# Self attention's projections in 16-bit float pairs, with scales found during cross attention, and the last FFN statistics ahead of the last products

## The reference, cut to what matters

```python
x = x + xattn(_layernorm(x), ctx, mask, rms_scale, q_w, kv_w, out_w)  # 4 heads of 128; keys and values from ctx (1601 rows)
x = x + attn(_layernorm(x), WQ, WK, WV, WO)                           # 16 heads of 32, causal, 64 rows
x = x + ffn(_layernorm(x), W_fc, ln_w, ln_b, W_proj)                  # ternary weights, GELU, layer norm over 2048
```

```python
def heads(W): return (x @ W).reshape(B, S, 16, 32).transpose(0, 2, 1, 3)
Q, K, V = heads(WQ), heads(WK), heads(WV)
score = einsum('bhqd,bhkd->bhqk', Q, K) / sqrt(32) + causal_mask
out = einsum('bhqk,bhkd->bhqd', softmax(score), V)
return out.reshape(B, S, E) @ WO
```

## Time and profile before

| | us |
|---|---|
| median of 3 runs | 1065.26 |
| the profiled execution, time | 1066.37 |
| the profiled execution, span of its trace | 1064.4 |
| PE busy / PEld busy | 930.7 / 700.7 |
| DVE busy / ACT busy / POOL busy | 668.4 / 505.0 / 375.6 |

### The profile page before, as it was taken

How to read it: one execution, slowest core, us unless ns; L and a number is a source line. 1 busy time by engine, 2 the same in 40 slices (tenths; PEclk the granted TensorE clock), 3 DMA queues, 4 the chain that set the end, 5 groups by cost and what they waited for, 6 DMA issues and landing times. The chain is left out here.

```text
span 1064.4 us, 22549 instructions
## 1 busy us (share of the span) xinstructions
PE 930.7 (87%) x7307; PEld 700.7 (66%) x7307; DVE 668.4 (63%) x1334; ACT 505.0 (47%) x1059; POOL 375.6 (35%) x506
## 2 busy tenths in 40 slices
PE   3798879898888888878979999999889999999996
PEld 2787667686676776657968887888765444444443
DVE  5577756766766777676366566766656538475543
ACT  4565445654455554544333333433446455555542
POOL 3354444444444444440022111211103325444434
PEclk9899989999999999988989999999989999999998
DMA  6621223211222322331355543444422102012011
GB/s 178 184 76 56 80 88 86 87 54 57 76 86 73 97 74 76 115 115 41 90 160 140 149 126 108 127 124 108 118 60 76 55 1 88 32 40 70 21 60 43
DMA packets 100318, 93.02 MB, mean 87 GB/s; under 512 B 45424, under 2 KB 61904, under 8 KB 100176
## 3 DMA queue, kind: packets, MB, share of 16 engines
q1 hardware_dynamic: 99376, 90.96, 29.2%
q10 hardware_dynamic: 672, 0.26, 0.1%
q0 software_dynamic: 128, 0.03, 0.0%
HBM read 74.37 MB, written 12.66 MB: 82 GB/s over the span
## 5 line engine op out<-in xcount | busy, mean ns | idle before, releaser
L255 PE MATMUL bank<-f,f 128*128 128x256 f32 (+4 forms) x5032 | 637.8, 300 | 68.8 <-issue 26.0
L255 PEld LDWEIGHTS bank<-f,f 128*128 128x128 f32 (+3 forms) x5032 | 460.9, 160 | 196.5 <-issue 80.8
L244 DVE TENSOR_TENSOR f<-bank,f 128x512 fp32r<-128x512 f32 x211 | 140.5, 683 | 47.7 <-ACT f L241 45.8
L241 ACT ACTIVATE f<-bank 128x512 fp32r<-128x512 f32 x211 | 121.1, 591 | 88.8 <-PE bank L230 83.6
L230 PE MATMUL bank<-f,f 128*128 128x128 f32 x896 | 132.5, 279 | 33.7 <-DVE f L244 13.0
L230 PEld LDWEIGHTS bank<-f,f 128*128 128x128 f32 x896 | 102.9, 143 | 56.1 <-issue 31.3
L1248 PE MATMUL bank<-f,f 128*128 128x512 f16 x512 | 123.1, 384 | 0.0
L1221 POOL TENSOR_TENSOR f<-f,f 128x512 f32<-128x512 f32 x59 | 75.1, 1273 | 132.9 <-ACT f L1216 132.9
L1226 DVE SCALAR_TENSOR_TENSOR f<-bank,f,f 128x512 f16<-128x512 f32 x64 | 48.0, 750 | 92.0 <-ACT f L1208 75.8
L463 POOL TENSOR_TENSOR f<-f,f 128x512 f32<-128x512 f32 x32 | 42.0, 1311 | 160.9 <-ACTq L75 138.9
L954 POOL TENSOR_TENSOR f<-f,f 128x512 f32<-128x512 f32 x32 | 33.4, 1043 | 177.4 <-DVE f L951 177.4
(11 more groups left out here) (138 smaller groups left out, 995.6 us busy)
## 6 DMA issues: line engine op xcount, KB each, us to landing
f<-in_ctx_dram SPq DMA_DIRECT2D x71, 256.0 KB, 2.8
f<-x_scratch SPq DMA_DIRECT2D x64, 256.0 KB, 3.8
x_scratch<-f SPq DMA_DIRECT2D x32, 256.0 KB, 2.0
f<-in_L_ffn_W_fc_dram SPq DMA_DIRECT2D x32, 256.0 KB, 2.9
f<-in_L_ffn_W_proj_dram SPq DMA_DIRECT2D x32, 256.0 KB, 3.4
f<-in_x_dram SPq DMA_DIRECT2D x31, 256.0 KB, 2.9
f<-in_ktab_dram SPq DMA_DIRECT2D x71, 64.0 KB, 2.0
f<-f SPq DMA_DIRECT2D x64, 64.0 KB, 2.4
```

What stands on the lines that cost most here:

```text
L241: return maybe("act", lambda e: e.activation(hi, src, ACT.Copy), sem(name + "_hi"), waits, when)
L244: return maybe("dve", lambda e: e.tensor_tensor(lo, src, hi.bitcast(F32), ALU.subtract), sem(name + "_lo"), waits, when)
L255: f = lambda e, i=i, a=a, b=b: e.matmul(dst, a, b, start=(first and i == 0), stop=(last and i == n - 1), skip_group_check=check)
```

## The change

Self attention's four weights, its turned x tiles (`XT`) and its attention output (`ET2`) become pairs of `float16`. A weight is first divided by its largest magnitude `m`, so that its low part stays in range: `hi = f16(w/m)`, `lo = w/m - hi`. Q and K are multiplied by `m` when they are copied from PSUM (`scale=wis` on an instruction that is there already); V stays scaled, and WO's product is multiplied by `m_V * m_O` in `store`, which adds the residual.

To find `m` each weight is loaded once more during cross attention, at slots 24, 38, 52 and 66, into `wo_t`. Four VectorE reductions in the slots s+4 to s+7 give the largest magnitude of each partition; it is written to DRAM (s+9), read back to all partitions (s+11), and reduced again and inverted (s+13). The split of a weight takes `scale=` on ScalarE, and on VectorE a scalar_tensor_tensor in place of a tensor_tensor; `store` takes a scalar_tensor_tensor too. The places in SBUF are laid out anew. The numbers of matmuls and their columns stay as they are.

At the end of the FFN the last group's statistics come before all products of the last two steps, the sums of squares first, and these products are then made row tile by row tile.

```diff
     for i in range(3):
-        Wh[i], Wl[i] = early(4, D, dt=F32R), early(4, D, dt=F32R)
-    XT = [early(2, 4, 256, dt=F32R), early(2, 4, 256, dt=F32R)]
+        early.at = CONST + (24576, 32768, 57344)[i]
+        Wh[i], Wl[i] = early(4, D, dt=F16), early(4, D, dt=F16)
+    XT = [early(2, 4, 256, dt=F16), early(2, 4, 256, dt=F16)]
-    Wh[3], Wl[3] = outs(4, D, dt=F32R), outs(4, D, dt=F32R)
+    Wh[3], Wl[3] = outs(4, D, dt=F16), outs(4, D, dt=F16)
-    ET2 = [late(4, 128, dt=F32R), late(4, 128, dt=F32R)]
+    ET2 = [late(4, 128, dt=F16), late(4, 128, dt=F16)]
...
+    def s2_wfetch(i):
+        w = (WK, WQ, WV, WO)[i]
+        tok["ws", i] = dma(wo_t[:, :, :], w.rearrange("(c p) n -> p c n", p=128), "s_wst",
+                           [*(tok["wm", i - 1] if i else ()), *tw1["o"]])
+    def s2_wmax(i, c):
+        t = op("dve", lambda e: e.tensor_reduce(wmc[:, c:c + 1], wo_t[:, c, :], AX.X, ALU.max, apply_absolute_value=True),
+               sem("s_wm"), [tok["ws", i]])
+        if c == 3:
+            t = op("dve", lambda e: e.tensor_reduce(wmx[:, i:i + 1], wmc[:, :], AX.X, ALU.max), sem("s_wm"), [t])
+            tok["wm", i] = [t]
+    def s2_wout(i):
+        tok["wo", i] = dma(wmaxd[i:i + 1, :].rearrange("a (p n) -> (a p) n", n=1), wmx[:, i:i + 1], "s_wmo", tok["wm", i])
+    def s2_wback(i):
+        tok["wb2", i] = dma(back[:, i, :], wmaxd[i:i + 1, :].to_broadcast([128, 128]), "s_wmb", [tok["wo", i], tok["tq"]])
+    def s2_wscale(i):
+        D_ = lambda f, w: op("dve", f, sem("s_wm"), w)
+        t = D_(lambda e: e.tensor_reduce(wis[:, i:i + 1], back[:, i, :], AX.X, ALU.max), [tok["wb2", i]])
+        t = D_(lambda e: e.tensor_scalar(wis[:, i:i + 1], wis[:, i:i + 1], 1.0e-30, None, ALU.max), [t])
+        t = D_(lambda e: e.reciprocal(wsc[:, i:i + 1], wis[:, i:i + 1]), [t])
...
     def s2_wsplit(i, after, c):
-        tW[i] = split("s_W2", raw_w(i)[:, c, :], Wh[i][:, c, :], Wl[i][:, c, :],
-                      [tok["w", i], *after()], [tok["w", i]])
+        th = op("act", lambda e: e.activation(hi, src, ACT.Copy, scale=wsc[:, i:i + 1]), sem("s_W2_hi"),
+                [tok["w", i], tok["wsc", i], *after()])
+        tl = op("dve", lambda e: e.scalar_tensor_tensor(lo, src, wsc[:, i:i + 1], hi, ALU.mult, ALU.subtract),
+                sem("s_W2_lo"), [th, tok["w", i], tok["wsc", i]])
+    def halves(name, src, hi, lo, w_hi, w_lo=()):
+        th = op("act", lambda e: e.activation(hi, src, ACT.Copy), sem(name + "_hi"), w_hi)
+        return th, op("dve", lambda e: e.tensor_tensor(lo, src, hi, ALU.subtract), sem(name + "_lo"), [th, *w_lo])
...
-        to = op("dve", lambda e: e.tensor_tensor(xo[:, u, :], bank[k][:, :], xr[:, u, :], ALU.add),
+        to = op("dve", lambda e: e.scalar_tensor_tensor(xo[:, u, :], bank[k][:, :], wsc[:, 4:5], xr[:, u, :],
+                                                        ALU.mult, ALU.add),
...
-        tok["qk", u] = [op("act", lambda e: e.activation(o, bank[k][:, 0:256], ACT.Copy), sem("a_QK"),
+        tok["qk", u] = [op("act", lambda e: e.activation(o, bank[k][:, 0:256], ACT.Copy, scale=wis[:, w:w + 1]), sem("a_QK"),
...
+    for i in range(4):
+        s = 24 + 14 * i
+        at(s, 9, lambda i=i: s2_wfetch(i))
+        for c in range(4):
+            at(s + 4 + c, 2.95, lambda i=i, c=c: s2_wmax(i, c))
+        at(s + 9, 9, lambda i=i: s2_wout(i))
+        at(s + 11, 9, lambda i=i: s2_wback(i))
+        at(s + 13, 2.95, lambda i=i: s2_wscale(i))
...
     def s3_plast():
-        for t in (2, 3):
-            s3_p(last - 1, [t])
         for t in range(4):
-            s3_p(last, [t])
+            for q in (last - 1, last):
+                s3_p(q, [t])
...
-        w = [*tok["acc", g], *tok["acc2", g], *gfree[k], t_on]
-        for t in range(4):
-            for z in range(2):
+        w = {1: [*tok["acc2", g], *gfree[k], t_on], 0: tok["acc", g]}
+        for z in (1, 0):
+            for t in range(4):
...
-    at(H0 + last + 2, 2.1, lambda: s3_p(last - 1, [0, 1]))
```

More of the change, by code:

```diff
@@ L166, in few @@
 def few(nc, handle, bank, base, x1d, x2d, x, ctxd, mask, rms, qw, kvw, ow, WQ, WK, WV, WO, Wfc, lnw, lnb,
-        Wproj, cosk, sink, cosq, sinq, identd, causald, out, picked, kmask, ktab, plan, nb=B):
+        Wproj, cosk, sink, cosq, sinq, identd, causald, out, picked, kmask, ktab, plan, wmaxd, nb=B):
     ni = nb // 2
@@ L754, in few @@
     for i in range(3):
-        Wh[i], Wl[i] = early(4, D, dt=F32R), early(4, D, dt=F32R)
-    XT = [early(2, 4, 256, dt=F32R), early(2, 4, 256, dt=F32R)]
+        early.at = CONST + (24576, 32768, 57344)[i]
+        Wh[i], Wl[i] = early(4, D, dt=F16), early(4, D, dt=F16)
+    early.at = CONST + 73728
+    XT = [early(2, 4, 256, dt=F16), early(2, 4, 256, dt=F16)]
+    early.at = CONST + 90112
     xa, xn = early(2, D), early(2, D)
-    Wh[3], Wl[3] = outs(4, D, dt=F32R), outs(4, D, dt=F32R)
+    Wh[3], Wl[3] = outs(4, D, dt=F16), outs(4, D, dt=F16)
     WO_raw = outs(4, D)
@@ L777, in few @@
     mrow, mdiag, isc, sc, lsc = const(2), const(2), const(2), const(2), const(2, 16)
+    wmc, wmx, wis, wsc = const(4), const(4), const(4), const(5)
+    back = Region(CONST + EARLY + 72704, CONST + EARLY + 74752)(4, 128)
     tok, tW = {}, {}
@@ new lines, in s2_wout @@
+    def s2_wout(i):
[7 more added lines that the diff above has]
+        t = D_(lambda e: e.reciprocal(wsc[:, i:i + 1], wis[:, i:i + 1]), [t])
+        if i == 3:
+            t = D_(lambda e: e.tensor_tensor(wsc[:, 4:5], wis[:, 2:3], wis[:, 3:4], ALU.mult), [t])
+        tok["wsc", i] = t
@@ L872, in ln_T @@
         tok["xnT", i] = [tt]
-        tok["XT", i] = split("n_XT", dst, dsth, dstl, [tt, *free])
+        tok["XT", i] = halves("n_XT", dst, dsth, dstl, [tt, *free])
         give(k, tok["XT", i])
@@ L878, in store @@
         u, j = i % 2, i % ni
-        to = op("dve", lambda e: e.tensor_tensor(xo[:, u, :], bank[k][:, :], xr[:, u, :], ALU.add),
-                sem("n_xo"), [tk, tok["xr", i], *tok["late"], *d2("ost", i - 2)])
+        to = op("dve", lambda e: e.scalar_tensor_tensor(xo[:, u, :], bank[k][:, :], wsc[:, 4:5], xr[:, u, :],
+                                                        ALU.mult, ALU.add),
+                sem("n_xo"), [tk, tok["xr", i], tok["wsc", 3], *tok["late"], *d2("ost", i - 2)])
         tok["out", i] = [to]
@@ L901, in s2_qk @@
         o = (QT, KT)[which][:, u % 2, c, :]
-        tok["qk", u] = [op("act", lambda e: e.activation(o, bank[k][:, 0:256], ACT.Copy), sem("a_QK"),
-                           [tk, *tW[w], *tok["early"], *d2("sc", 2 * u - 3)])]
+        tok["qk", u] = [op("act", lambda e: e.activation(o, bank[k][:, 0:256], ACT.Copy, scale=wis[:, w:w + 1]), sem("a_QK"),
+                           [tk, tok["wsc", w], *tW[w], *tok["early"], *d2("sc", 2 * u - 3)])]
         give(k, tok["qk", u])
@@ L1002, in s2_ET @@
         tok["enT", i] = [tt]
-        tok["ET", i] = split("a_ET", dst, ET2[0][:, :, :], ET2[1][:, :, :], [tt, *tok["late"], *d2("o2", i - 1)])
+        tok["ET", i] = halves("a_ET", dst, ET2[0][:, :, :], ET2[1][:, :, :], [tt, *tok["late"], *d2("o2", i - 1)])
         give(k, tok["ET", i])
@@ L1281, in s3_stat @@
                         bank[k][:, z * 4 + t:z * 4 + t + 1], a, ones[:, 0:1], start=n == 0, stop=n == m,
-                        skip_group_check=True), sem("f_p") if t == 3 and z and n == len(parts) - 1 else None,
-                        w if t + z == 0 else ())
+                        skip_group_check=True), sem("f_p") if t == 3 and not z else None,
+                        w[z] if t + n == 0 else ())
         tok["stat", g] = [tk]
@@ L2452, in program @@
         places = nc.dram_tensor("tile_rows", (B, FT), I32, kind="Internal").ap()
+        wmaxd = nc.dram_tensor("weight_max", (4, 128), F32, kind="Internal").ap()
         handles = []
@@ L2476, in program @@
                identd, causald, out)
-        short, prep, steps, ahead, begun = few(nc, semaphores(8), bank, base, x1d, x2d, *ins, picked, kmask, ktab, plan)
+        short, prep, steps, ahead, begun = few(nc, semaphores(8), bank, base, x1d, x2d, *ins, picked, kmask, ktab, plan,
+                                               wmaxd)
         long = every(nc, semaphores(0, begun), bank, base, x1d, x2d, *ins)
```

3 lines of the change are left out of this document (added).

## The result

The changed kernel takes 1072.91 us (median of 4 runs, 1071.1 to 1073.77); the kernel before, on the same chip, 1064.98 (4 runs, 1063.77 to 1065.47). The ratio is 1.0074, 95% interval 1.0056 to 1.0091: slower by 0.7%, where 1055.4 us, 0.9% faster, was forecast. The profiled execution took 1072.21 us with a span of 1070.1.

A forecast was written before the change was run, and what follows sets the result against it. TensorE, the busiest engine in every stretch, was taken as the bound, by its own pace in self attention's steady part. Profiled 1066.4 - 12.2 + 3 - 0.7 = 1056.5 us, median 1.1 lower: 1055.4 us, range 1050 to 1062.5.

The forecast's parts named there:

- What self attention's matmuls save: Self attention: float16 starts 0.108 and 0.216 us apart; 8.4 us (bounds 0 and 8.4) with 256 columns, 6.9 with 512.
- the 15.3 us: Self attention: TensorE time saved by float16 matmuls with 256 and 512 columns together, bounds 6.9 and 15.3.
- the 1067.6: Time by the skill's pace formula, self attention already at its floor and nothing gained; under a rival with chance 0.10.
- How much arrives: Self attention: half of the ramp's saving, nine tenths of the steady part's 12.3 us, less 0.4 at half clock: 12.2 us.
- the ramp: Start of self attention, 484 to 556 us: half of 3.0 us saved counts, 1.5 us, since other engines' chains hold TensorE.
- ScalarE's `scale=`: Scaling put on existing ScalarE instructions in self attention: adds no instruction, so no cost was counted.
- the lower bound: Self attention's least arriving gain, with 512 columns alone and the same shares: 5 us.
- What the search costs: Cross attention: 14.2 us of added VectorE work, mostly hidden, costs 3 us (bounds 0 and 14.2); transfers cost 0.
- The trip through DRAM: Cross attention: write, landing and read back hidden, 3.2 us for the read against 7 us of lead; cost 0.
- rival (c): Cross attention: late SP transfers make the inversion hold VectorE four times; at 4 us each, 1071 us; chance 0.06.
- Rival (b): Cross attention: VectorE's new work lands on TensorE's path nearly in full, 12 us of 14.2, giving 1064.4; chance 0.08.
- The end: End of the FFN: statistics start about 0.7 us sooner, gaining 0.7 us (bounds 0 and 0.75).

The follow-up runs named there:

- e2: The kernel before plus the search alone, its result unused, with float32r pairs and the old end: 1077.02 us, ratio 1.0110.
- e6: The kernel before with only the new order of its end: 1064.69 us beside 1064.62, ratio 0.9997.
- e1: The changed kernel without the search (no second load, reductions or trip through DRAM), scales set by constants: 1057.05 us, 0.9919 of the kernel before.
- e4: The changed kernel with second load and reductions but no write, read back or inversion, scales constant: 1060.09 us, 0.9948 of the kernel before.
- e5: The changed kernel with second load and trip through DRAM but no reductions, writing a constant 0.25: 1062.75 us, 0.9967 of the kernel before.
- e7: The changed kernel with only the inversion moved, from s+13 to s+19: 1063.84 us, 0.9972 [0.9956, 0.9987] of the kernel before.
- e0: The changed kernel itself, unaltered, timed again in another comparison: 1067.28 us, 1.0019 of the kernel before.
- e9: The changed kernel with the read back moved to s+22 and the inversion to s+32: 1062.77 us, 0.9967 of the kernel before.
- e16: The changed kernel without the search, scales constant, run again in a later comparison: 1058.13 us, 0.9932 of the kernel before.
- e15: The changed kernel without the search, scales constant, and with the old end: 1057.03 us, 0.992 of the kernel before.
- e3: The changed kernel with the read back moved to s+14 and the inversion to s+19: 1063.44 us, 0.9979 of the kernel before.
- e11: e4 plus the four writes of 128 x 4 bytes to DRAM, nothing read back: 1060.67 us, 0.9962 of the kernel before.
- e10: The changed kernel without the trip, maximum over partitions by TensorE transpose and matmul in slot 84: 1066.83 us, 1.0015 of the kernel before.

## Why the prediction was wrong, step by step

**What self attention's matmuls save: right.** 0.109 and 0.216 us against 0.108 and 0.216. The choice between the bounds 0 and 8.4 us for 256 columns was right, and with it the 15.3 us. The formula of the Trainium skill ("TensorE: Matmul & The Clock Gate", Back-to-back issue gap), which is given there for isolated matmuls, 109 and 216 ns, agrees with these rows for `float16`; for `float32r` it did not. The time lies nearer to the 1067.6 by it than to my forecast, but by luck: the paces did fall as forecast, and what took the gain away is the search.

**How much arrives: the share was too high, and the half clock takes part of it.** 12.2 us were forecast and 0.7 for the end; 8.9 arrived from slot 127 to the end in the profiled execution, and that holds the new end. Behind slot 127 the kernel before has 43.3 us at half clock and the changed one 48.1, so up to 2.4 of the 4.0 missing us are clock. It isn't chance alone: every one of the fifteen traces with `float16` pairs has a half-clock stretch of 3.4 us some 26 to 28 us behind slot 127 (after: from 517.1), and none of the three with `float32r` (before, `e2`, `e6`) has one there. What stands ahead of it is a wait for the high half of a weight, 2.1 us in the fifteen and 1.7 in the three.

The kernels with fixed scales give 0.9919 and 0.9932 in all, 7.2 to 8.6 us. I had written that a wait behind a transpose "moves with TensorE" and doesn't eat what was saved. The waits in the twelve tiles grew from 15.1 to 19.9 us instead. My reading is that such a wait is a chain of fixed length through ScalarE and VectorE, partly covered by TensorE's products that stand between transposes and use: the products got shorter, the chain didn't (the two halves of such a split take 0.59 and 0.68 us on ScalarE and VectorE before and after). Only 1.4 of the 4.8 us stand in rows that name a split, though; for the 2.3 in the row "issue" the cause isn't shown. The share was 6.6 of 11.5, not nine tenths.

In the ramp, from slot 127 to the scores of the second tile, I counted 1.5 us and nothing arrived (86.5 us before, 87.0 after), with 19.7 us at half clock before and 24.1 after: the difference, 2.2 us when halved, is more than what was forecast there.

ScalarE's `scale=` was priced at nothing because it "adds no instruction"; it does make the instructions longer. The copies of Q and K, before and after:

```profile
L902 ACT ACTIVATE f<-bank 128x256 f32<-128x256 f32 x64 | 24.3, 380 | 81.9 <-PE bank L255 81.3
```

```profile
L945 ACT ACTIVATE f<-bank,f 128x256 f32<-128x256 f32 x64 | 30.0, 469 | 75.8 <-PE bank L255 75.8
```

That is 0.09 us for each of 64, and as much for each high half of a weight (0.62 to 0.71 us); the low half takes 0.83 us on VectorE instead of 0.69, where 0.06 more was forecast. What of it reaches TensorE isn't shown.

One sum of this step is wrong, without consequence: the lower bound, 512 columns alone with these shares, is 0.4 + 5.4 - 0.4 = 5.5 us and not 5.

**What the search costs: the step that failed.** It was priced at 3 us: 16 reductions and four inversions at 0.15 us each, the transfers at nothing. Measured, the search costs 10.7 us alone (`e2`), and the changed kernel's ratios, 1.0019 and 1.0074, stand 0.0100 and 0.0155 above `e1`'s 0.9919: 10.7 to 16.5 us. Three terms stand in its place.
- The reductions: 10.9 us of VectorE as forecast, and `e4` less `e1` is 0.0029, 3 us (`e4`'s waits: +3.6). Forecast were 2.4 us (16 x 0.15), so this term was about right.
- The trip through DRAM, its transfers taken as hidden and priced at nothing: +4.6 us of TensorE's waits (`e5`). I had written "cost 0, and if that cover is gone, VectorE stands and waits, with all behind it". The cover was gone. I counted one landing, the read's 3.2 us, against 7 us of lead; the write lands 8.2 us (median) after its issue and the read 4.1 after its own, and SP waits in between. At the worst place the read back went out at 314.50 and VectorE stood waiting for it from 318.73 - 2.50 = 316.23: 1.7 us of lead, not 7. Moving the inversion alone by six slots (`e7`) took 3 to 4 us of waits away and brought the ratio from 1.0019 to 0.9967. This is rival (c)'s mechanism, with a smaller size at VectorE (4.8 us in all) than its price of 4 us for each of four.
- The half clock, not forecast in cross attention at all: up to 4.6 us between the two profiled executions (half of 23.7 - 14.4). The worst stall, 4.06 us with 6.8 us at half clock, goes with a late landing of the write (9.5 us); where it landed after 7.4 the wait was 1.62 us and the clock stayed full (`e0`).

Rival (b)'s 12 us came out as a total, but not by its mechanism: the reductions cost a quarter of it.

**The end: right in the trace, nothing in the time.** The statistics moved by 0.73 us and the end of the span by 0.6; neither pair of kernels shows it in the time, where less than 0.2% can't be told apart.

**What stays open.** `e9` has no wait of VectorE for the read back and still stands 0.0031, 3 us, above `e4`, with +1.7 us of TensorE's waits; write and read alone cost no more than the intervals allow. Whether the remainder is the sum of small terms or the half clock's placement wasn't settled. The second load was never run alone. Nor was it settled why the changed kernel differs by half a per cent between two comparisons, beyond the landing and the half clock named above.

The best version is the one with fixed scales (`e1`, `e16`, with the old end `e15`): 0.992 to 0.993 of the kernel before. It gives up that the scale follows the weights. Of those that find the magnitudes themselves, `e7` with 0.9967 has the lowest ratio, though `e3` and `e9` can't be told from it: it is the change with one number altered, s + 19 for s + 13.

## What to carry to other kernels

When an engine that sets the time gets faster, look at each of its waits and ask what covered the chain behind it: a wait for a chain of fixed length can grow by what was saved between the chain's start and its use. A round trip through DRAM is two landings (8.2 and 4.1 us here) and the issuing queue's own waits, so give its consumer that much lead in slots, above all where the consumer stands in a queue that is first in, first out. And before new work goes in front of a clock-sensitive engine, count its waits and its time at half clock apart: here their sum explained the length of every one of the 18 traces within 3 us.

## What the runs showed of the hardware

- 128 numbers of four bytes, one from each partition, took 7.3 to 8.2 us (median) from issue to landing in DRAM, about as long as a 1 MB weight load (some 6 to 8 us in the same traces). The Trainium skill, "DMA: Bandwidth & Descriptors", section Specifications, puts the size for full rate at 512 bytes or more; the direction agrees, and the 8 us are this trace's. The same page, section "Anatomy of one DMA — SWDGE (gpsimd) path", says of transfers issued by GpSimd that their completion can be surprisingly late when the target is HBM. For SyncE's writes that isn't what sets the 8 us: 256 KB written to DRAM (`x_scratch`) land in 2.0.
- Such a write holds up what is issued behind it on the same queue. Of two x loads of 256 KB at the same place of the program, both land in 4.1 us (median) without the write (`e4`, at 299.8). With it between them (`e11`) the first lands in 3.9 and the second, issued 0.5 us behind the write, in 9.4; in the changed kernel it is 4.1 and 11.8, and the mask behind takes 9.9.
- Every stall of TensorE of more than 3 us in cross attention has a stretch at 1.2 GHz with it. In four of five the clock fell 1.2 to 1.6 us before the stall ended: 4.06 us and 6.8 us at half clock (after, from 322.6), 3.31 and 6.8 (`e2`, from 320.3), 3.63 and 10.2 (`e10`, from 327.9), 3.60 and 6.8 (`e5`, from 159.1). In the fifth, 3.25 us in `e0`, which ended at 160.85, it fell at 162.3, for 3.4 us. A stall of 2.85 us (`e5`, until 317.81) had none, and stretches of 3.4 us at half clock come without such a stall too (before, at 139.7, 150.0 and 266.0; the longest stall of that trace up to 469 us is 1.4).
- With `float16` pairs a 128x256 matmul starts every 0.109 us and a 128x512 one every 0.216; with 32-bit pairs it was 0.119 and 0.234. At half clock the type makes no difference: 0.214 with 32-bit pairs and (567.37 - 566.52)/4 = 0.213 with `float16`, both with 256 columns, by these rows of TensorE's order of time in the changed kernel:

```profile
566.52 2.34 PE L255 MATMUL bank<-f,f 128*128 128x256 f16 x10
...
567.37 1.48 PE L255 MATMUL bank<-f,f 128*128 128x256 f16 x6
```
